# Expert blocks in pairs, register loads by fours, and the planner's charge for a turn set to zero, in a fused cross-attention and mixture-of-experts kernel

## The chip, the cores and the metric

The kernel runs on one core of one Trainium2 chip, in one launch. The metric is device time in microseconds (us). Three runs of the kernel before took 674.27, 676.44 and 676.86 us; the median is 676.44.

## What is computed

2048 tokens of 256 features (fp32) attend to 1601 context rows in 16 heads of 16 features, then go through a mixture of eight experts, two of which serve each token.

```
x = x + xattn(layernorm(x), ctx, ctx, mask)
    q, k, v = query @ Wq.T, key @ Wk.T, value @ Wv.T           # 16 heads, dk = 16
    attn    = softmax(q k^T / 4, masked, causal)
    output  = sigmoid(query @ Wg.T + bg) * (attn @ v) @ Wo.T
x = x + ffn(layernorm(x))
    top 2 of softmax(x @ gate_w) per token give scale[T, 8]
    xs = scale.T[:, :, None] * x                               # (8, T, 256)
    y  = (silu(xs @ w1) * (xs @ w3)) @ w2                      # hidden size 128
    out = y.sum(over experts)
```

## The kernel before, in words

**Attention.** Tokens are worked in four chunks of 512, in the order 1, 2, 3, 0, and each chunk in four groups of four heads; that makes 16 passes n. A pass has three kinds of product on TensorE (PE). *Maximum pieces* (`mx`, L1702, with the causal mask added by small products, L1706) give scores with the queries on the partitions; VectorE (DVE) reduces each to a row maximum (L1392). The maxima of a pass are folded (`mred`, `mT`: POOL, PE, ACT, a small DMA) into an extra row of the queries. *Score products* (`st`, L1735, mask L1740) then give the scores with the keys on the partitions, less the maximum, and ScalarE (ACT) takes their exponential into `probs` (L1267). There are 592. Both kinds run as pairs: two heads in the two halves of PE's rows. *Value products* (`pv`, L1757) take four heads at once, in four strips of 32 columns, and sum over the keys in one bank. A unit is one pass's block of 128 keys; `probs` has room for two units. Of a unit of 512 queries the values are two shares of 256, each of four products.

**Router.** When a chunk's passes are done, `gT`, `wo`, a second layernorm, `xT1` and `logits` (L1585 with `gw_sb`) give the expert scores; DVE ranks them, `cnt` counts rows per expert, `wide` scales each row for its two experts, and POOL scatters the rows into the DRAM table `sent` (`scat`, L1120), sorted by expert. SP writes zero rows behind each expert's last row (`tail`, L986 to L989). Chunks 1, 2, 3 are set 0, chunk 0 is set 1.

**Expert blocks.** 128 rows of one expert are a block: 31 in set 0 and 15 in set 1, 46 in all. Which expert a block belongs to is known only at run time, so SP and PE load it into a register (`value_load`, L1003 and L1824). A block has six steps: `bl`, SP loads the rows (L1004) into one of four places of `row_in`; `bx`, PE transposes them (L1819), ACT copies the high part (L1284), DVE takes the low part (L1548); `bab`, six products with w1 and w3 (L1835 to L1837), ACT takes tanh (L1290), DVE forms the hidden rows (L1554, L1556); `bh`, one transpose (L1843) and again a high and a low part; `by`, three products with w2 (L1849 to L1851), copied out by ACT (L1302); `bst`, SP stores to `fed` (L1010). The steps of four blocks are interleaved by `LAGS`: in round i stand bx(i), bab(i-1), bh(i-2), by(i-3).

**The end.** When all blocks of a set are stored, POOL gathers for each half chunk of 256 tokens the two result rows of every token (`back`, four gathers, L1137) into one of three places `got` in `gate_sb`; DVE adds them to x (`add`, L1569, L1570), and SP stores (`out`, L1015).

**Order.** `make_plan` (L265) walks all steps once with costs in ns, always takes the step that could start first (rounded by TOLERANCE, ties by a deadline in which `PATIENCE` enters), and so writes one list from which each engine takes its own steps in that order. The deciding lines:

```
        if mode != mode_of(e):
            at += SWITCH
...
                key = (max(0, round((at - last) / TOLERANCE)), deadline(name, e, at))
```

The mode is "scores" for `st` and `mx`, "values" for `pv`, "other" for the rest. SP's and POOL's steps are sorted by the times at which the plan has them begin. `needs` lists what each step waits for in the plan.

## Time and profile before

| | |
|---|---|
| median of three runs | 676.44 us |
| profiled execution | 673.26 us, span 671.5 |
| PE busy | 589.1 us, 88% of the span |
| DVE busy | 476.6 us, 71% |
| ACT busy | 382.9 us, 57% |
| POOL busy | 220.0 us, 33% |
| DMA | 51.03 MB, mean 76 GB/s |
| DVE row maxima, L1392 | 323.0 us busy, 640 instructions |
| ACT exponentials, L1267 | 281.7 us busy, 592 instructions |

A busy PE is not PE at its peak: its products overlap, and the end of each is modelled and includes a tail. So distances between the starts of products tell more than their lengths. Idle time of an engine that isn't the bottleneck costs nothing. In the views, PEld is PE's weight load, and a time in brackets is the idle time before an instruction with what released it ("issue": nothing that the profile shows).

### The profile page before, as it was taken

Reading aid. Unit: us, or ns where it says so; the run is one execution under the profiler, and the core shown is the slowest. Engines: PE = TensorE matmul, PEld = TensorE weight load, DVE = VectorE, ACT = ScalarE, POOL = GpSimd, SP = SyncE. Lnnn points to the kernel's source line nnn. Section 1 sums busy time; section 2 is a strip of 40 time slices with the busy share of each in tenths; the row PEclk is TensorE's granted clock in tenths of the full one; section 3 lists DMA queues with packets and bytes.
Section 4 is the critical chain, followed back from the end, with each engine's and each line's share of the span. In section 5 each row is a group of like instructions: output and inputs, shape, how many; then the busy total and the mean of one; then the engine's idle time right before and its main releaser. Section 6 shows DMA issues by size and latency. Waiting matters only on the chain.

```text
span 671.5 us, 14892 instructions
## 1 busy us (share of the span) xinstructions
PE 589.1 (88%) x5272; PEld 353.4 (53%) x5272; DVE 476.6 (71%) x1167; ACT 382.9 (57%) x882; POOL 220.0 (33%) x306
## 2 busy tenths in 40 slices
PE   8896999999999999999999999988898586788750
PEld 3363565555565545554565555533355374777640
DVE  6636779998979999989898896810024678565651
ACT  2221456676656577766756668789977233455430
POOL 6004311432123575030104085477021502100754
PEclk9879799999999999999999899999999799799995
DMA  6985882010170010010087010000000324544873
GB/s 170 231 134 104 142 153 40 2 22 2 65 95 2 2 56 11 1 53 13 3 93 189 3 48 19 4 2 2 1 2 9 134 80 148 177 141 142 223 210 109
DMA packets 43554, 51.03 MB, mean 76 GB/s; under 512 B 8073, under 2 KB 32777, under 8 KB 43482
## 3 DMA queue, kind: packets, MB, share of 16 engines
q1 hardware_dynamic: 37416, 40.50, 26.6%
q0 software_dynamic: 5120, 8.66, 4.5%
q8 instruction: 44, 0.72, 0.5%
q10 hardware_dynamic: 946, 0.92, 0.4%
q14 instruction: 28, 0.23, 0.1%
HBM read 27.41 MB, written 20.58 MB: 71 GB/s over the span
## 4 chain that ended last, share of the span: by engine, by line
PE 27%; DVE 15%; ACT 9%; issue 5%; POOL 3%; DMA 2%; SPq 1%; POOLq 0%; DVEq 0%; ACTq 0%
DVE pmax L1392 9%; ACT probs L1267 7%; PE bank L1757 7%; PE bank L1735 5%; PE bank L1585 3%; PE bank L1702 3%; PE bank L1835 2%; POOL gate_sb L1137 2%; DMA gate_sb<-fed,back_at 1%; PE bank L1837 1%; PE bank L1836 1%; ACT y_sb L1302 1%; POOL sent L1120 1%; DMA fed<-y_sb 1%; PE bank L1706 1%
## 5 line engine op out<-in xcount | busy, mean ns | idle before, releaser
L1267 ACT ACTIVATE probs<-bank 128x512 f32<-128x512 f32 (+4 forms) x592 | 281.7, 560 | 123.9 <-PE bank L1735 77.8
L1392 DVE TENSOR_REDUCE pmax<-bank 128x1 f32<-128x512 f32 (+6 forms) x640 | 323.0, 575 | 29.9 <-PE bank L1706 15.4
L1757 PE MATMUL bank<-probs,vaug 128*32 128x256 f32 (+4 forms) x2048 | 144.5, 394 | 7.9 <-ACT probs L1267 6.3
L1735 PE MATMUL bank<-qaug,kaug 64*128 64x512 f32 (+4 forms) x592 | 146.9, 452 | 2.6 <-DVE pmax L1392 0.9
L1702 PE MATMUL bank<-kaug,qaug 62*128 62x512 f32 (+6 forms) x640 | 137.8, 405 | 10.0 <-ACT rest L1205 4.2
L1735 PEld LDWEIGHTS bank<-qaug,kaug 64*128 64x128 f32 (+1 forms) x592 | 63.8, 183 | 81.1 <-ACT probs L1267 31.6
L1702 PEld LDWEIGHTS bank<-kaug,qaug 62*128 62x128 f32 x640 | 76.9, 190 | 43.2 <-DVE pmax L1392 20.9
L1757 PEld LDWEIGHTS bank<-probs,vaug 128*32 128x32 f32 (+1 forms) x2048 | 52.6, 110 | 60.4 <-ACT probs L1267 26.6
L1137 POOL DMA_INDIRECT gate_sb<-fed,back_at x32 | 31.6, 986 | 59.2 <-DMA fed<-y_sb 46.4
L1835 PE MATMUL bank<-w_hi,row_hi 128*128 x92 | 31.5, 342 | 16.2 <-ACT y_sb L1302 6.5
L1162 POOL DMA_DIRECT2D qaug<-m_row x64 | 34.7, 548 | 31.9 <-ACT m_row L1274 31.9
L1407 DVE TENSOR_SCALAR rsum<-bank 128x16 f32<-128x16 f32 x16 | 2.7, 167 | 53.5 <-PE bank L1767 53.5
L1080 POOL TENSOR_TENSOR rstd<-var_e,minus_half 128x4 f32<-128x4 f32 x8 | 8.3, 1042 | 91.8 <-DVE var_e L1352 91.7
L1706 PE MATMUL bank<-tri_b,eye_b 64*128 64x128 bf16 (+1 forms) x416 | 36.8, 225 | 0.0
L1176 POOL TENSOR_TENSOR att_sb<-att_sb,gate_sb 128x256 f32<-128x256 f32 x16 | 11.7, 731 | 76.2 <-DVE att_sb L1412 75.7
L1290 ACT ACTIVATE t_sb<-bank 128x128 f32<-128x128 f32 x46 | 12.8, 277 | 41.6 <-PE bank L1837 41.6
L1149 POOL TENSOR_SCALAR nmax<-rmax 128x16 f32<-128x16 f32 x16 | 4.4, 277 | 89.9 <-DVE rmax L1400 89.5
L1835 PEld LDWEIGHTS bank<-w_hi,row_hi 128*128 128x128 f32 x92 | 18.3, 199 | 25.8 <-issue 25.7
L1554 DVE SCALAR_TENSOR_TENSOR at_sb<-t_sb,bank 128x128 f32<-128x128 f32 x46 | 13.1, 286 | 24.7 <-ACT t_sb L1290 24.7
L1200 ACT ACTIVATE stage<-bank 128x512 fp32r<-128x512 f32 (+1 forms) x16 | 8.8, 551 | 36.1 <-PE bank L1585 27.9
L1740 PE MATMUL bank<-eye_b,tri_b 64*128 64x64 bf16 (+1 forms) x416 | 27.5, 195 | 0.0
L1284 ACT ACTIVATE row_hi<-bank 128x256 fp32r<-128x256 f32 x46 | 17.4, 380 | 16.8 <-PE bank L1819 16.7
(178 smaller groups left out, 823.2 us busy)
## 6 DMA issues: line engine op xcount, KB each, us to landing
row_in<-sent SPq DMA_DIRECT2D x46, 128.0 KB, 2.1
fed<-y_sb SPq DMA_DIRECT2D x46, 128.0 KB, 2.1
qaug<-q_parts SPq DMA_DIRECT2D x18, 256.0 KB, 8.4
q_parts<-stage SPq DMA_DIRECT2D x7, 512.0 KB, 2.9
sent<-none_sb SPq DMA_DIRECT2D x18, 128.0 KB, 1.8
k_parts<-stage SPq DMA_DIRECT2D x4, 512.0 KB, 5.0
w_sb<-in_w SPq DMA_DIRECT2D x4, 512.0 KB, 10.3
out<-x_sb SPq DMA_DIRECT2D x8, 256.0 KB, 3.2
```

The costliest lines, as they stand in the source:

```text
L1137: pool.indirect_dma_start(got[:, g % GOT, k, t, :], None, rows, bass.IndirectOffsetOnAxis(ap=back_at[:, k, 2 * g + t:2 * g + t + 1], axis= ...
L1162: pool.dma_start(qaug[row:row + 1, p % 2, GP * g:GP * (g + 1), :].bitcast(F32), m_row[at:at + GP, :].bitcast(F32)).then_inc(m_landed[n % 4 ...
L1267: act.activation(probs[0:rows, u % NSLOT, h, off:CH], bank_of(e)[0:rows, off:CH], ACT.Exp, scale=DK ** -0.5).then_inc(act_read, 1)
L1284: act.activation(row_hi[:, i % 2, :], bank_of(e)[:, 0:D], ACT.Copy).then_inc(row_hi_ready, 1)
L1392: dve.tensor_reduce(pmax[:, n % 2, qt, h, slot:slot + 1], bank[:, 0:w], AX_X, ALU.max).then_inc(dve_read, 1)
L1585: last = pe.matmul(dst, lhs(a), rhs(a), start=(a == 0), stop=(a == KD - 1))
L1702: last.append(pe.matmul(pair[side][0][:, 0:w], qaug[b:b + ROW_MAX, p % 2, hp, P * qt:P * (qt + 1)], keys_at(b, ROW_MAX, hp, k0, w), start= ...
L1706: last = [pe.matmul(bank[:, d:w], eye_b[b:b + HALF, a + 1 - side, :], tri_b[b:b + HALF, a + 1 - side, 0:w - d], start=False, stop=(a == 1) ...
L1735: last.append(pe.matmul(pair[side][0][0:r, off:CH], keys_at(b, ROWS, hp, P * j, r), qaug[b:b + ROWS, p % 2, hp, off:CH], start=True, stop= ...
L1740: last = [pe.matmul(bank[0:r, q0:q0 + HALF], tri_b[b:b + HALF, a + 1 - side, 0:r], eye_b[b:b + HALF, a + 1 - side, HALF * a:HALF * (a + 1) ...
L1757: last = pe.matmul(psum[O_BANK][32 * h:32 * h + 32, q0:q1], vaug[0:r, col:col + 32], probs[0:r, u % NSLOT, h, q0:q1], start=(j == 0), stop ...
L1835: pe.matmul(bank[:, 0:D], high, hi, start=(a == 0), stop=False)
```

## The change

- **Blocks in pairs.** Two neighbouring blocks of a set (31 blocks become 15 pairs and a single, 15 become 7 and a single, so 24 steps for 46 blocks) share a bank, a wait and each ACT and DVE instruction. PE's products stay as many. Rings hold two pairs (`RING` = 2), row places `XIN` are two pairs, `YOUT` three pairs. Row places move into `gate_sb`. One store writes both blocks. Row loads stay one per block.
- **Registers by fours.** `named` loads four table entries with one instruction, on SP and on PE, where each block had its own.
- **Gathers.** Four landing places instead of three, in the space of `probs`; the first gather waits for the last value product.
- **Late additions.** `PATIENCE` gets an entry of 30000 for the additions.
- **The planner's costs.** `SWITCH`, the charge for a change of mode, goes from 100 to 0; costs of pairs, of scatters and gathers are new; the weights' split (`ws`) no longer waits in the plan for the last pass's maxima.

```diff
-RELOAD, SWITCH, HOP, LOAD, PIECE = 107, 100, 2500, 9000, 3000
+RELOAD, SWITCH, HOP, LOAD, PIECE = 107, 0, 2500, 9000, 3000
-PATIENCE = {"turn": 1000, "route": 3000, "project": 6000, "weights": 0, "blocks": 4000}
+PATIENCE = {"turn": 1000, "route": 3000, "project": 6000, "weights": 0, "blocks": 4000, "adds": 30000}
-BLOCKS = [(s, b) for s, count in enumerate(COUNT) for b in range(count)]
+PAIRS = [(s, b, min(2, count - b)) for s, count in enumerate(COUNT) for b in range(0, count, 2)]
+NAMED = 4
-XIN, YOUT, GOT = 4, 3, 3
+XIN, YOUT, GOT, RING = 2, 3, 4, 2
-THEN = {"stat": 1050, "mred": 1100, "mT": 2300, "ws": 2700, "gm": 750, "norm": 4900, "scat": 8800, "back": 4400, "wide": 9800}
+THEN = {"stat": 1050, "mred": 1100, "mT": 2300, "ws": 2700, "gm": 750, "norm": 4900, "scat": 10400, "back": 5200, "wide": 9800}
         if kind == "ws":
-            return [("prologue_end",), ("mred", NC * G - 1)] + all_st(freed_by(e[1]))
+            return [("prologue_end",)] + all_st(freed_by(e[1]))
-        got = gate_sb[:, 1:NC, :].rearrange("p g (k t d) -> p g k t d", k=2, t=2)
+        got = words[:, 0:GOT * 4 * D].rearrange("p (g k t d) -> p g k t d", g=GOT, k=2, t=2)
+        row_in = gate_sb[:, ORDER[0], :].rearrange("p (i k d) -> p i k d", i=XIN, k=2)
+        def named(table, s, b, engine, most):
+            count = min(NAMED, COUNT[s] - b)
+            _, values = nc.values_load_multi_w_load_instructions(table[0:1, s, b:b + count], engines=[engine], min_val=0, max_val=most,
+                                                                 skip_runtime_bounds_check_because="the table's values are bounded by its last step")
+            return {(s, b + k): value for k, value in enumerate(values)}
...
+        def landed(i):
+            return row_landed[i % XIN], 16 * sum(PAIRS[o][2] for o in range(i % XIN, i + 1, XIN))
@@ SP, bl @@
                     if i == 0:
-                        sp.wait_ge(*made(last_st[last_unit[G * (NC - 1) - 1]]))
+                        sp.wait_ge(*made(("logits", ORDER[0])))
                     if i >= XIN:
-                        sp.wait_ge(*taken(("bx", i - XIN)))
-                    at = sp.value_load(read_i[0:1, s, b:b + 1], min_val=0, max_val=E * ROOM[s])
-                    sp.dma_start(row_in[:, i % XIN, :], sent[s][bass.ds(at, 1), :, :].rearrange("r p d -> (r p) d")).then_inc(row_landed[i % XIN], 16)
+                        sp.wait_ge(*made(("bx", i - XIN)))
+                    if b % NAMED == 0:
+                        from_row.update(named(read_i, s, b, mybir.EngineType.SP, E * ROOM[s]))
+                    for k in range(n):
+                        sp.dma_start(row_in[:, i % XIN, k, :], sent[s][bass.ds(from_row[s, b + k], 1), :, :].rearrange("r p d -> (r p) d")
+                                     ).then_inc(row_landed[i % XIN], 16)
@@ SP, bst @@
-                    sp.dma_start(fed[s][b, :, :], y_sb[:, i % YOUT, :]).then_inc(y_stored[i % YOUT], 16)
+                    sp.dma_start(fed[s][b:b + n, :, :].rearrange("r p d -> p r d"), y_sb[:, i % YOUT, 0:n, :]).then_inc(y_stored[i % YOUT], 16)
@@ POOL, back @@
                     if g == 0:
-                        for o in ORDER[0:NC - 1]:
-                            pool.wait_ge(*made(("logits", o)))
+                        pool.wait_ge(pv_done, len(units))
@@ ACT, bx; bab, bh and by are changed in the same way @@
-                    act.activation(row_hi[:, i % 2, :], bank_of(e)[:, 0:D], ACT.Copy).then_inc(row_hi_ready, 1)
+                    act.activation(row_hi[:, i % RING, 0:n * D], bank_of(e)[:, 0:n * D], ACT.Copy).then_inc(row_hi_ready, 1)
@@ PE, bab @@
-                    pe.wait_ge(*taken(("bx", i)))
+                    if b % NAMED == 0:
+                        whose.update(named(whose_i, s, b, mybir.EngineType.PE, E - 1))
+                    pe.wait_ge(*taken(("bx", i)))
                     bank = make(e)
-                    for a in range(KD):
+                    for k in range(n):
+                        dst = bank[:, D * k:D * (k + 1)]
+                        for a in range(KD):
...
```

The plan moves the attention's steps against each other. On PE, in the middle of the attention, just ahead of the transposes of the eleventh fold (`nmax_b`), before. Scores and maxima (`kaug` with `qaug`) take two products for a pair, values (`vaug`) four for a share.

```order
L1757 MATMUL bank<-probs,vaug 32x256 x8
L1735 MATMUL bank<-qaug,kaug 128x512 x2
L1702 MATMUL bank<-kaug,qaug 128x364 x4
L1735 MATMUL bank<-qaug,kaug 128x512 x2
L1757 MATMUL bank<-probs,vaug 32x256 x8
L1735 MATMUL bank<-qaug,kaug 128x512 x2
L1702 MATMUL bank<-kaug,qaug 128x512 x4
L1735 MATMUL bank<-qaug,kaug 128x512 x2
L1757 MATMUL bank<-probs,vaug 32x256 x8
L1735 MATMUL bank<-qaug,kaug 128x512 x2
L1702 MATMUL bank<-kaug,qaug 128x364 x4
L1715 MATMUL bank<-eye_b,nmax_b 8x128 x4
```

The same place in the changed kernel (score products are now L1761, maximum pieces L1728 with mask L1732, values L1783):

```order
L1728 MATMUL bank<-kaug,qaug 128x364 x2
L1732 MATMUL bank<-tri_b,eye_b 128x65 x4
L1783 MATMUL bank<-probs,vaug 32x256 x4
L1761 MATMUL bank<-qaug,kaug 128x512 x2
L1728 MATMUL bank<-kaug,qaug 128x512 x2
L1783 MATMUL bank<-probs,vaug 32x256 x4
L1728 MATMUL bank<-kaug,qaug 128x512 x2
L1761 MATMUL bank<-qaug,kaug 128x512 x2
L1728 MATMUL bank<-kaug,qaug 128x364 x2
L1783 MATMUL bank<-probs,vaug 32x256 x4
L1761 MATMUL bank<-qaug,kaug 128x512 x2
L1741 MATMUL bank<-eye_b,nmax_b 8x128 x4
```

The two value shares of a unit are apart now, and maximum pairs stand singly. Over the whole of PE's order the mode changes 557 times where it changed 375 times; 508 of the 592 score products and 896 of the 1024 value products stand ahead of the last maximum piece, where 432 and 748 stood; and behind the logits of chunk 3 stand 12 score products, where 28 stood.

On PE, one round of the expert blocks, before (no row is left out between two register loads):

```order
L1824 TENSOR_LOAD whose_i
L1824 ISA x2
L1835 ISA [waits act_read,dve_read]
L1835 MATMUL bank<-w_hi,row_hi 128x256
L1836 MATMUL bank<-w_hi,row_lo 128x256
L1837 REGISTER_ALU
L1837 MATMUL bank<-w_lo,row_hi 128x256
L1835 ISA
L1835 MATMUL bank<-w_hi,row_hi 128x256
```

and now, where a second pair ends its transposes (the rounds between two such loads have none):

```order
L1847 MATMUL bank<-ident,gate_sb 128x128 [waits dve_read,row_landed1]
L1847 MATMUL bank<-ident,gate_sb 128x128 x3
L861 TENSOR_LOAD whose_i
L1866 ISA [waits act_read,dve_read]
L1866 MATMUL bank<-w_hi,row_hi 128x256
L1867 MATMUL bank<-w_hi,row_lo 128x256
L1868 REGISTER_ALU
L1868 MATMUL bank<-w_lo,row_hi 128x256
L1866 ISA
```

The load of a register (TENSOR_LOAD with two ISA rows) stands once per four blocks, without the two rows behind it.

On SP, in the same stretch, before:

```order
L1003 TENSOR_LOAD read_i [waits dve_read]
L1003 ISA x2
L1004 ISA
L1004 DMA row_in<-sent 128x256
L1010 DMA fed<-y_sb 128x256 [waits act_read]
```

and now, a round with and a round without a register load:

```order
L861 TENSOR_LOAD read_i [waits dve_full]
L1026 ISA
L1026 DMA gate_sb<-sent 128x256
L1026 ISA
L1026 DMA gate_sb<-sent 128x256
L1033 DMA fed<-y_sb 128x2x256 [waits act_read]
L1026 ISA [waits dve_full]
L1026 DMA gate_sb<-sent 128x256
L1026 ISA
L1026 DMA gate_sb<-sent 128x256
L1033 DMA fed<-y_sb 128x2x256 [waits act_read]
```

Two row loads and one store of twice the size stand where two loads and two stores stood, and the loads wait for the transposes (`dve_full`) instead of DVE's copy (`dve_read`).

## Rows read from the trace of the kernel before

**Rows 1.** Windows: length, busy us of each engine, PEclk, DMA share, GB/s.
```profile
300.00:400.00 100.00, 97.32 (x864) 54.22 (x862) 91.38 (x208) 63.12 (x130) 24.84 (x35) 0.98 0.30 58
...
438.00:490.00 52.00, 45.72 (x536) 19.55 (x534) 2.40 (x9) 50.09 (x105) 24.94 (x25) 1.00 0.01 2
...
583.00:617.00 34.00, 29.26 (x215) 25.20 (x214) 21.08 (x72) 19.40 (x72) 0.00 (x0) 1.00 0.46 140
```

**Rows 2.** Page, groups: busy us, mean ns, idle before; the exponentials.
```profile
L1267 ACT ACTIVATE probs<-bank 128x512 f32<-128x512 f32 (+4 forms) x592 | 281.7, 560 | 123.9 <-PE bank L1735 77.8
```

**Rows 3.** Timeline of PE, 243 to 254 us: start, length, instructions.
```profile
244.64 0.49 PE L1735 MATMUL bank<-qaug,kaug 64*128 64x512 f32 x2
245.06 1.07 PE L1757 MATMUL bank<-probs,vaug 128*32 128x256 f32 x16
246.06 0.50 PE L1735 MATMUL bank<-qaug,kaug 64*128 64x512 f32 x2
...
251.41 0.50 PE L1735 MATMUL bank<-qaug,kaug 64*128 64x512 f32 x2
251.75 0.56 PE L1702 MATMUL bank<-kaug,qaug 62*128 62x512 f32 x4
252.18 0.90 PE L1735 MATMUL bank<-qaug,kaug 64*128 64x512 f32 x2
253.08 1.07 PE L1757 MATMUL bank<-probs,vaug 128*32 128x256 f32 x16
```

**Rows 4.** Groups of PE by line, 97 to 438 us.
```profile
L1702 PE MATMUL bank<-kaug,qaug 62*128 62x512 f32 (+6 forms) x560 | 117.3, 396 | 2.4 <-DVE pmax L1392 1.0 <-DVE new_sum L1496 0.4
L1735 PE MATMUL bank<-qaug,kaug 64*128 64x512 f32 (+4 forms) x420 | 113.3, 461 | 2.6 <-DVE pmax L1392 0.9
L1757 PE MATMUL bank<-probs,vaug 128*32 128x256 f32 (+4 forms) x1456 | 101.6, 391 | 0.1
L1706 PE MATMUL bank<-tri_b,eye_b 64*128 64x128 bf16 (+1 forms) x336 | 28.0, 220 | 0.0
```

**Rows 5.** Timelines of DVE at 437 us and of ACT at 525 us.
```profile
437.37 1.29 DVE L1392 TENSOR_REDUCE pmax<-bank 128x1 f32<-128x512 f32 x2 [0.25 <-PE bank L1706]
...
524.73 1.08 ACT L1267 ACTIVATE probs<-bank 128x256 f32<-128x256 f32 x5
```

**Rows 6.** Timelines of PE, POOL and SP, 508 to 536 us.
```profile
508.74 1.95 PE L1585 MATMUL bank<-gw_sb,gate_sb 128*128 128x8 f32 x16
...
522.66 1.16 POOL L1120 DMA_INDIRECT sent<-att_t,slots  x1 [0.26 <-DVE row_sb L859]
...
535.11 11.91 SPq L1004 DMA_DIRECT2D row_in<-sent  x8
```

**Rows 7.** Chain that ended last: start, length, engine.
```profile
584.52 0.38 PE bank L1835
...
607.70 0.37 PE bank L1835
```

**Rows 8.** Timeline of PE and its weight loads, one block.
```profile
590.23 0.38 PE L1835 MATMUL bank<-w_hi,row_hi 128*128 x1 [0.21 <-ACT y_sb L1302]
...
591.49 0.39 PE L1819 MATMUL bank<-ident,row_in 128*128 128x128 f32 x2
...
592.15 0.19 PEld L1835 LDWEIGHTS bank<-w_hi,row_hi 128*128 128x128 f32 x1 [0.52 <-issue]
```

**Rows 9.** Timeline of SP: tail rows written ahead of further loads.
```profile
565.55 8.51 SPq L989 DMA_DIRECT2D sent<-none_sb  x8
```

**Rows 10.** Timelines of POOL (gathers) and SP (last store).
```profile
620.05 0.99 POOL L1137 DMA_INDIRECT gate_sb<-fed,back_at  x1 [45.20 <-DMA fed<-y_sb]
...
655.60 0.94 POOL L1137 DMA_INDIRECT gate_sb<-fed,back_at  x1 [4.84 <-issue]
...
664.64 0.95 POOL L1137 DMA_INDIRECT gate_sb<-fed,back_at  x1 [0.30 <-issue]
...
668.97 0.37 SPq L1015 DMA_DIRECT2D out<-x_sb  x1
```

More of the change, by code:

```diff
@@ L193, in block_steps @@
 def block_steps():
-    steps, count = [], len(BLOCKS)
+    steps, count = [], len(PAIRS)
     for i in range(count + max(LAGS.values())):
@@ L245, in read_time @@
         return per[0] * max_pieces(e[1])[e[2]][3] + per[1]
-    if kind in ("v", "logits", "by"):
+    if kind == "by":
+        return per[0] * PAIRS[e[1]][2] * D + per[1]
+    if kind in ("v", "logits"):
         return per[0] * D + per[1]
@@ L282, in make_plan @@
         "weights": [[("ws", ex)] for ex in range(E)],
-        "loads": [[("bl", i)] for i in range(len(BLOCKS))],
+        "loads": [[("bl", i)] for i in range(len(PAIRS))],
         "blocks": [[e] for e in block_steps()],
-        "stores": [[("bst", i)] for i in range(len(BLOCKS))],
+        "stores": [[("bst", i)] for i in range(len(PAIRS))],
         "backs": [[("back", *o)] for o in halves()],
@@ L462, in alone @@
         if kind in THEN:
[L463 removed]
+            at = on_pool(e, at) + (1.5 * HOP if kind in ("scat", "back") else 60)
         elif kind in ("kload", "qload"):
```

137 lines of the change are left out of this document (77 added, 60 removed).

## The prediction

> **What bounds the kernel now.** I read the windows first, then the timeline of PE, then the chain that ended last. The kernel has two halves. In the attention half (until 526 us) two thirds of the time lie under the row maxima: from 300 to 400 us PE is busy 97.3 of 100 us and DVE 91.4, while ACT, which has all the exponentials, is busy 63.1 [rows 1]. Once the last maximum is taken (DVE, 437 us) ACT alone sets the pace: 50.1 of 52 us busy, DVE 2.4 [rows 1, 5]. So exponentials that could have run under the maxima run behind them, until 526 us [rows 5]. The second half is the expert blocks. From 584.52 to 607.70 twelve blocks pass on the chain, 1.93 us each [rows 7]. PE needs 1.26 us from a block's first product (590.23) to the next transposes (591.49). Of the 0.67 us that remain its weight load stands idle for 0.52, released by nothing but "issue" [rows 8]; I count 0.44 as a gap and 0.23 as the two transposes, so 1.49 of work. The gap lies where PE fetches the block's expert number into a register. From 620 us POOL gathers the results, and the end hangs on its last gather at 664.64 and the last store at 668.97 [rows 10].
>
> **The attention's order.** No instruction of attention is added; the planner's charge for a turn between tilings went from 100 to 0. Counted from the order of instructions, PE has 557 turns where it had 375, and 508 of the 592 score products (148 more of the 1024 value products too) now stand ahead of the last maximum, where 432 stood.
>
> 1. Behind the last maximum ACT has 76 exponentials less, at 0.56 us [rows 2]: -42.5 us.
> 2. Ahead of it PE has 38 score pairs more at 0.34 us (251.41 to 251.75) and 37 groups of four value products at 0.50 (245.06 to 246.06 is two groups) [rows 3]: 12.9 + 18.5 = +31 us.
> 3. A turn: a score pair takes 0.34 us before a maximum and 0.42 before values (244.64 to 245.06) [rows 3], 0.08 more. The turn back is inside the 1.00 us of the values; I take 0.09 for both, 182 x 0.09 = +16 us.
> 4. Two maximum pairs in a row take 0.43 us, 0.215 each, and next to another kind 0.34, the score pair's price [rows 3]; 64 such neighbourhoods are gone: 64 x 0.125 = +8 us.
> 5. Against these 55 us stands the room PE has under the maxima. Between 97 and 438 us, 341 us, stand 182 value groups (eight records each) x 0.50, 210 score pairs x 0.34 and 280 maximum pairs x about 0.27, between 0.215 and 0.34: 238 us [rows 4]. The other groups of that view (the masks on L1706 are the largest) add up to 85 us busy [rows 4], with each one's tail counted; as distances some 60. That leaves about 43 us of waiting; 252.18 to 253.08 shows a piece of it, 0.90 us where 0.42 would do [rows 3]. A new order can use between none and all 43. I take 30, since more alternation gives PE a ready product more often: -30 us.
>
> So the last exponential moves by -42.5 + 55 - 30 = -17.5 us; between the ends of the room from +12.5 to -30.5.
>
> The Trainium skill's page "TensorEngine Tiling (Array Packing)", section Key Properties, says that a change of tiling mode drains TensorE, which speaks against this edit. The page "TensorE: Matmul & The Clock Gate" puts a drain near 175 ns; by it an estimate for item 3 is 32 us in place of 16, and the whole sum would come out 16 us longer.
>
> 6. The way from the router's last big step to the first row load: logits of chunk 3 at 508.74, first scatter 522.66, first row load 535.11 [rows 6]. Before, 28 exponentials stand behind those logits, now 12. The way of 26 us stays as long, and 16 exponentials at about 0.53 us less lie beside it. So row loads come 8 us later after the last exponential: +8 (0 to +9). Queued there are POOL's scatters, SP's tail rows, and all blocks.
>
> Attention together -9.5 us (-30 to +21). The splitting of the expert weights on POOL is moved ahead of several folds; I cost it at nothing, since a fold's maxima lead its scores by 30 or more exponentials, over 15 us. If that cover is gone, PE waits at the first scores of a unit, some 5 us.
>
> **The blocks.** 46 blocks become 24 steps: same products, half of the ACT and DVE instructions, and one register load per four blocks on PE and SP.
>
> 7. A pair costs PE 2 x 1.49 us, and the 0.44 us gap falls on every second pair: 3.18 us where two blocks took 3.86, -0.68. ACT needs at most 2 x 19.4/18 = 2.2 us and DVE 2.3, even unpaired [rows 1]; neither becomes the bound. Set 0 has 15.5 pairs: -10.5 us. Bounds: nothing (the gap only moves), and -13.6 (no gap at all, 15.5 x 0.88).
> 8. SP still puts nine tail writes of set 1, 8.51 us for eight of them [rows 9], ahead of later row loads, and four blocks of row buffers are all the cover as before: 0. The row buffer comes free at its transposes instead of after DVE's copy, and two loads are issued for it instead of one; both beside PE's two steps, so 0, for as long as SP keeps up (a rival below).
> 9. The end. The first gather is at 620.05, the last at 664.64; POOL stands between at 655.60 for the stores of set 1 and for additions [rows 10]. Gathers come every 1.25 us when nothing holds them, 32 of them in all. With four landing places and set 1 ready in time, the last starts at 620.05 + 31 x 1.25 = 658.8: -5.8 us. Set 1 has eight more steps plus a store, about 8 x 3.18 + 3 = 28 us after set 0's last; POOL reaches its gathers 33 us after it. So set 1's blocks hide under the gathers, and so do the late additions; nothing is booked for them. Bounds: 0 and -5.8. What is late next is POOL itself.
>
> Blocks together -16 us (-4 to -19).
>
> **Sum.** -9.5 - 16 = -25.5 us. The profiled execution took 673.26 us with a span of 671.5; the median of the runs shown is 676.44, 3.2 above it. The span should be 646, the profiled time near 648 and the median 651.
>
> **Rivals.**
> *Rows too late.* A pair's loads wait for the transposes two steps back and land some 2 us after issue; if SP, which also stores, comes late, PE waits each step and item 7 is gone: -9.5 - 5.8, 661 us. For it: DMA gaps on PE exist at the blocks' start. Against: two steps of 3.2 us for it, and fewer SP instructions. The same time comes out if the register load simply costs as much on the pairs as before; then the change wouldn't do what it says.
> *No gain in attention.* PE uses only 10 of the 43 us of room: +10.5 - 16, 671 us. For it: PE is busy 97.3 of 100 us already, and the windows can't tell a wait from a product's tail.
> *Turns make PE the bound, slower.* One mechanism: each turn empties the array and nothing overlaps it. Its price at most is the full distance from 0.215 us (a pair in a run) to 0.42: 0.205 a turn, 182 x 0.115 = 21 us more than item 3, and no room used: 12.5 + 21 + 8 - 16 = +25.5, 702 us. At 0.09 a turn it decides only if less than 1 us of room is used (then 681); at 0.205 if less than 22 us is. For it: PE's share. Against: the tight 0.42 in the trace, with the turn in it.
>
> **How the numbers follow.** A measurement of this kernel can tell about 0.5%, 3.4 us, from no change. Forecast 0.58, with its own range of 636 to 664. Late rows 0.12 (661). No gain in attention 0.16 (671, from 666 to 680, so a third of it within 0.5%). Turns 0.12 (680 to 702), nearly all of it slower. Better than forecast (all 43 us of room) 0.02. Faster: 0.58 + 0.12 + 0.08 + 0.02 = 0.80; same 0.08; slower 0.12. The range from 634 to 678 leaves out the turns above 678 and a little below.
>
> **What would show it.** Last maximum near 463 us (later than 437), last exponential near 508, first row load near 526, the chain's blocks 3.2 us a pair with an "issue" gap every second pair, first gather near 600, and 32 gathers without a break longer than 2 us. The forecast is wrong if the last exponential comes later than 520, if the score pair before values takes much over 0.42 us where PE waits for nothing, if a block pair takes over 3.6 us, or if POOL waits on stores of set 1.

## The result, and the profile after

The changed kernel takes 657.06 us (median of 4 runs, 654.97 to 663.90) against 675.36 us before (4 runs, 672.60 to 676.86): ratio 0.9706, interval 0.9647 to 0.9764. It is faster by 18.3 us where 25.4 were forecast. The profiled one of these four runs (663.90 us) was slowed by a lower clock, so the profile read here is that of a second, unaltered run of it (e1 below), with a span of 653.4 us where before had 671.5, and ratios and intervals go by undisturbed runs alone.

The page of it, first parts (columns as for the kernel before):

```profile
span 653.4 us, 14223 instructions
PE 573.5 (88%) x5272; PEld 328.7 (50%) x5272; DVE 473.2 (72%) x1079; ACT 377.8 (58%) x794; POOL 219.6 (34%) x306
PEclk8799999999999799999999889999999869979955
```

PE has the same 5272 products, ACT has 794 instructions. The windows that answer to [rows 1]: a stretch under the maxima, the stretch from the last maximum to the last exponential, and one of steady blocks.

```profile
300.00:400.00 100.00, 95.88 (x862) 48.49 (x858) 84.52 (x187) 67.52 (x131) 38.74 (x45) 0.95 0.32 70
467.60:512.00 44.40, 41.24 (x524) 23.83 (x516) 10.36 (x35) 35.45 (x90) 9.66 (x13) 1.00 0.01 3
583.00:603.00 20.00, 19.82 (x157) 19.21 (x157) 11.48 (x26) 11.65 (x28) 0.00 (x0) 0.94 0.52 164
```

The numbers are those of PE, PEld, DVE, ACT and POOL, then PE's granted clock (PEclk), the DMA share and GB/s. In the second line ACT is busy 35.5 of 44.4 us. Before it had 50.1 of 52: ACT no longer sets the pace alone. In the third, PE is busy 19.8 of 20 us (before 29.3 of 34): PE now bounds the blocks.

The marks of the forecast in the timelines (start, length): DVE's last maximum and ACT's last exponential [rows 5], then logits of chunk 3, first and last of its eight scatters, first row load [rows 6].

```profile
466.66 1.29 DVE L1415 TENSOR_REDUCE pmax<-bank 128x1 f32<-128x512 f32 x2 [0.51 <-PE bank L1732]
...
512.02 0.79 ACT L1289 ACTIVATE probs<-bank 128x128 f32<-128x128 f32 x4 [0.18 <-PE bank L1766]
```
```profile
505.84 1.95 PE L1611 MATMUL bank<-gw_sb,gate_sb 128*128 128x8 f32 x16
...
518.10 1.22 POOL L1143 DMA_INDIRECT sent<-att_t,slots  x1 [1.67 <-DVE row_sb L878]
...
527.23 0.96 POOL L1143 DMA_INDIRECT sent<-row_sb,slots  x1 [0.30 <-issue]
...
530.28 13.63 SPq L1026 DMA_DIRECT2D gate_sb<-sent  x12
```

The last maximum moved from 437.4 to 466.7 us, the last exponential from 525.8 to 512.8, the logits only from 508.7 to 505.8, and the first row load only from 535.1 to 530.3. The 24.4 us between logits and row load (26.4 before) are nearly a fixed way, with hardly anything of the exponentials in it: ACT's one small step there, `r_exp` at 509.82, stands behind four of them that start at 508.32.

Steady blocks, timeline of PE: the first transposes of two steps in a row and the first product of each, then the weight load of a step with a register load in front of it [rows 8]:

```profile
586.30 0.60 PE L1847 MATMUL bank<-ident,gate_sb 128*128 128x128 f32 x4
586.66 0.36 PE L1866 MATMUL bank<-w_hi,row_hi 128*128 x1
...
589.09 0.60 PE L1847 MATMUL bank<-ident,gate_sb 128*128 128x128 f32 x4
589.45 0.36 PE L1866 MATMUL bank<-w_hi,row_hi 128*128 x1
```
```profile
592.21 0.19 PEld L1866 LDWEIGHTS bank<-w_hi,row_hi 128*128 128x128 f32 x1 [0.17 <-issue]
```

A pair takes 2.79 us (586.66 to 589.45) where two blocks took 3.86, and before the weight load 0.17 us is left of the 0.52. But the steps aren't steady all the way. SP's queue between 560 and 600 us, and what PE waits for there (us in total, times, longest), first now, then before:

```profile
568.59 0.41 SPq L1006 DMA_DIRECT2D sent<-none_sb  x1
570.04 8.20 SPq L1009 DMA_DIRECT2D sent<-none_sb  x8
578.91 0.90 SPq L1026 DMA_DIRECT2D gate_sb<-sent  x2
```
```profile
PE bank L1847 <- DMA gate_sb<-sent: 7.4, 2, 7.2
```
```profile
PE bank L1819 <- DMA row_in<-sent: 2.1, 1, 2.1
```

The tail writes of set 1 stand ahead of a row load as in [rows 9]. PE waits 7.2 us for that load, where in the kernel before it waited 2.1. POOL's gathers and the tail of SP's queue [rows 10]:

```profile
606.46 0.99 POOL L1159 DMA_INDIRECT probs<-fed,back_at  x1 [27.45 <-DMA fed<-y_sb]
...
630.51 1.45 POOL L1159 DMA_INDIRECT probs<-fed,back_at  x1 [0.30 <-issue]
...
646.14 0.95 POOL L1159 DMA_INDIRECT probs<-fed,back_at  x1 [0.30 <-issue]
```

They run without the stop of 4.84 us that stood before the 25th. The saving by stretch, from the two traces:

| stretch, us | before | changed | difference |
|---|---|---|---|
| start to first row load | 535.1 | 530.3 | -4.8 |
| first row load to first gather | 84.9 | 76.2 | -8.7 |
| first gather to the end | 51.5 | 46.9 | -4.6 |
| span | 671.5 | 653.4 | -18.1 |

These are single executions. How far a mark moves with nothing changed ahead of it is shown by e5 below: its attention has the order of the kernel before, and its first row load stands at 537.5 us, 2.4 later. So the first line can be told to 2 or 3 us only.

### The profile page after: what moved, and what is told of

It is laid out like the page before. It is cut to its first block, busy times and chain, and to the rows that moved or that the text cites. A ratio compares the mean times of both kernels' runs of the same rounds, so it can differ in the third digit from the quotient of the medians.

```text
span 662.1 us, 14223 instructions
## 1 busy us (share of the span) xinstructions
PE 581.6 (88%) x5272; PEld 332.6 (50%) x5272; DVE 473.3 (71%) x1079; ACT 377.9 (57%) x794; POOL 220.1 (33%) x306
## 4 chain that ended last, share of the span: by engine, by line
PE 65%; DVE 10%; POOL 6%; issue 6%; DMA 4%; ACT 4%; SPq 4%; POOLq 0%; DVEq 0%; ACTq 0%
PE bank L1783 18%; PE bank L1761 13%; PE bank L1728 12%; PE bank L1611 9%; DVE pmax L1415 5%; ACT probs L1289 3%; POOL probs L1159 2%; PE bank L1732 2%; POOL row_sb L1115 1%; PE bank L1866 1%; PE bank L1847 1%; DMA probs<-fed,back_at 1%; PE bank L1868 1%; PE bank L1867 1%; PE bank L1687 1%
## 5 line engine op out<-in xcount | busy, mean ns | idle before, releaser
L1783 PE MATMUL bank<-probs,vaug 128*32 128x256 f32 (+4 forms) x2048 | 161.0, 404 | 3.1 <-ACT probs L1289 1.4
L1761 PE MATMUL bank<-qaug,kaug 64*128 64x512 f32 (+4 forms) x592 | 143.9, 450 | 7.4 <-DVE new_sum L1519 2.7
L1728 PE MATMUL bank<-kaug,qaug 62*128 62x512 f32 (+6 forms) x640 | 140.4, 423 | 3.5 <-DVE stage L889 1.9
L1761 PEld LDWEIGHTS bank<-qaug,kaug 64*128 64x128 f32 (+1 forms) x592 | 64.7, 188 | 77.9 <-DVE pmax L1415 26.1
L1728 PEld LDWEIGHTS bank<-kaug,qaug 62*128 62x128 f32 x640 | 69.9, 190 | 59.4 <-DVE pmax L1415 21.5
L1783 PEld LDWEIGHTS bank<-probs,vaug 128*32 128x32 f32 (+1 forms) x2048 | 46.0, 110 | 54.6 <-issue 26.5
L1159 POOL DMA_INDIRECT probs<-fed,back_at x32 | 31.6, 987 | 36.4 <-DMA fed<-y_sb 27.3
L1732 PE MATMUL bank<-tri_b,eye_b 64*128 64x128 bf16 (+1 forms) x416 | 32.4, 226 | 0.0
L1198 POOL TENSOR_TENSOR att_sb<-att_sb,gate_sb 128x256 f32<-128x256 f32 x16 | 11.8, 737 | 59.4 <-DVE att_sb L1435 57.6
L1306 ACT ACTIVATE row_hi<-bank 128x512 fp32r<-128x512 f32 (+1 forms) x24 | 13.7, 576 | 30.9 <-PE bank L1847 30.8
L1611 PE MATMUL bank<-wo_sb,att_t 128*128 128x256 f32 x64 | 17.2, 418 | 12.7 <-DVE att_t L1404 12.7
L1143 POOL DMA_INDIRECT sent<-att_t,slots x16 | 16.2, 1013 | 31.3 <-DVE row_sb L878 26.8
L1868 PE MATMUL bank<-w_lo,row_hi 128*128 x92 | 26.5, 288 | 0.0
L1867 PE MATMUL bank<-w_hi,row_lo 128*128 x92 | 26.4, 287 | 0.0
L1570 DVE TENSOR_TENSOR row_lo<-bank,row_hi 128x512 fp32r<-128x512 f32 (+1 forms) x24 | 15.9, 665 | 11.5 <-PE bank L1847 6.4
```

Source lines behind the costliest of these rows:

```text
L1159: pool.indirect_dma_start(got[:, g % GOT, k, t, :], None, rows, bass.IndirectOffsetOnAxis(ap=back_at[:, k, 2 * g + t:2 * g + t + 1], axis= ...
L1611: last = pe.matmul(dst, lhs(a), rhs(a), start=(a == 0), stop=(a == KD - 1))
L1728: last.append(pe.matmul(pair[side][0][:, 0:w], qaug[b:b + ROW_MAX, p % 2, hp, P * qt:P * (qt + 1)], keys_at(b, ROW_MAX, hp, k0, w), start= ...
L1732: last = [pe.matmul(bank[:, d:w], eye_b[b:b + HALF, a + 1 - side, :], tri_b[b:b + HALF, a + 1 - side, 0:w - d], start=False, stop=(a == 1) ...
L1761: last.append(pe.matmul(pair[side][0][0:r, off:CH], keys_at(b, ROWS, hp, P * j, r), qaug[b:b + ROWS, p % 2, hp, off:CH], start=True, stop= ...
L1783: last = pe.matmul(psum[O_BANK][32 * h:32 * h + 32, q0:q1], vaug[0:r, col:col + 32], probs[0:r, u % NSLOT, h, q0:q1], start=(j == 0), stop ...
```

## The experiments

Twelve runs were made in three batches, each beside the kernel before (medians 675.32, 675.10 and 675.09 us). The stretches of all of them stand in one table behind the runs; each reading below uses it.

**The changed kernel once more** (e1). No edit.

> The changed kernel unaltered, for a profile whose clock is not disturbed: in the first profile of it PE stood at half clock from 229 to 239 and from 273 to 280 us, in the middle of the attention. Theory (the order of the attention gains a little, the blocks most): 650 to 657 us, last exponential near 513 to 516, first row load near 531 to 533 against 535.1 before, first gather near 607. Rival (the half clock is what the new order brings itself, since PE waits differently): half clock in the attention again, 662 us.

Measured: 657.73 us, ratio 0.9742 (0.9706 to 0.9779). It repeats the result and gives the profile above. The rival's time didn't come, but its half clock did in part: PE's granted clock is at half (1.2 GHz) in this trace too, for 17.1 us between 100 and 467 us (23.9 in the first profile, 3.4 in the kernel before). Windows of 200 to 240 and 350 to 400 us, granted clock in the third number from the end:

```profile
200.00:240.00 40.00, 38.84 (x375) 20.17 (x374) 34.32 (x80) 25.14 (x53) 19.20 (x21) 0.91 0.01 5
350.00:400.00 50.00, 46.24 (x424) 22.40 (x416) 44.96 (x102) 34.38 (x64) 29.05 (x29) 0.90 0.22 65
```

**The order alone, both ways** (e2, e3). The planner's charge for a turn put back in the changed kernel, and taken from the kernel before:

```diff
-RELOAD, SWITCH, HOP, LOAD, PIECE = 107, 0, 2500, 9000, 3000
+RELOAD, SWITCH, HOP, LOAD, PIECE = 107, 100, 2500, 9000, 3000
```

> The changed kernel with the planner's charge for a turn back at 100: PE's order of the attention is again nearly the old one (374 turns, 434 of 592 score products ahead of the last maximum). Theory (items 1 to 6 of the forecast, attention -9.5): 5 to 12 us slower than the changed kernel, 662 to 667, last exponential near 526. Rival 'no gain in attention': within 3 us of the changed kernel. Rival 'turns make PE the bound': faster than the changed kernel.

Measured: 664.12 us, 0.9819 (0.9797 to 0.9841). As the theory said, the order is worth something in the changed kernel: 6.4 us, and the intervals of e1 and e2 don't touch; the first row load is at 537.1 with the old charge and at 530.3 with the new.

> The kernel before with the charge at 0 alone: 552 turns, 516 of 592 score products ahead of the last maximum, blocks single as before. Theory: faster than before by what the order is worth, 5 to 10 us (665 to 670). Rival 'no gain in attention': 673 to 677. Rival 'turns': slower, over 680.

Measured: 680.95 us, 1.0101 (1.0067 to 1.0134). The same number makes the kernel before slower by 5.6 us. That is the time which the rival of the turns gave, but its mechanism isn't what the trace shows. The last exponential does come earlier, 516.8 us instead of 525.8, but the logits of chunk 3 come later, 513.6 instead of 508.7. The chain that ended last says where they were held (start, length, what):

```profile
488.87 1.81 POOL w_lo L1106
490.68 0.77 POOL w_hi L1104
491.61 1.69 issue
493.29 0.73 POOL att_sb L1176
494.07 1.97 PE bank L1775 x8
496.04 3.71 PE bank L1585 x8
```

POOL splits the eight experts' weights (`w_hi`, `w_lo`), and the product that chunk 3's output waits for (`att_sb`, 493.29) stands behind them in its queue. Groups of POOL, 470 to 496 us, of this run:

```profile
L1106 POOL TENSOR_TENSOR w_lo<-w_sb,w_hi 128x768 fp32r<-128x768 f32 x8 | 14.5, 1812 | 0.6
L1104 POOL CAST w_hi<-w_sb 128x768 fp32r<-128x768 f32 x8 | 6.6, 825 | 0.0
```

That is 21 us in one block, 472.0 to 493.3 us, right behind the last maxima. In the kernel before the planner lets no split go ahead of the last pass's maxima; with the old charge these end at 438 us, with the new one at 465. The change drops that rule, and in the changed kernel the splits run at 369.8, 409.5 and 444.5 us, ended by 452.6. DVE had written what that product reads long before:

```profile
476.85 0.42 DVE L1412 TENSOR_TENSOR att_sb<-bank,rinv 128x256 f32<-128x256 f32 x1
```

It waited 16 us behind the splits. In the changed kernel POOL takes the same step at 483.27, 0.1 us after DVE is done with it. The wait also costs clock: the eight products of `wo` behind it take 3.71 us (496.04), and eight of the same kind 1.92 in the changed kernel (488.00). So the forecast's free side edit is, by these traces, what lets the order pay. It is read from the traces; the changed kernel with the old rule wasn't tried, so this is argued and not shown.

**Registers by fours** (e4, e5). Taken from the changed kernel, and given to the kernel before with its single blocks. Core of the first (SP's queue; PE's the same way):

```diff
-                    if b % NAMED == 0:
-                        from_row.update(named(read_i, s, b, mybir.EngineType.SP, E * ROOM[s]))
+                    for k in range(n):
+                        from_row[s, b + k] = sp.value_load(read_i[0:1, s, b + k:b + k + 1], min_val=0, max_val=E * ROOM[s])
```

> The changed kernel with a register load of its own for each block, as before, on SP and PE; pairs stay. Theory (item 7: the gap behind a register load is 0.44 us of every 1.93, and a pair has two of them again): up to 0.88 us per pair and 0.66 more than with one load in four blocks, 15.5 pairs, +5 to +10 us. Rival (the pairs' shared ACT and DVE instructions are what made the step shorter, the register load is hidden): within 2 us of the changed kernel.

Measured: 667.70 us, 0.9874 (0.9845 to 0.9903): 10 us lost, all of it between first row load and first gather (85.7 us against 76.2). Of PE's weight loads after 585 us, this is what one behind the register loads looks like:

```profile
590.11 0.29 PEld L1866 LDWEIGHTS bank<-w_hi,row_hi 128*128 128x128 f32 x1 [1.11 <-issue]
```

Two loads for a pair leave a gap of 1.11 us here (behind a wait, at the lower clock), and between 0 and 1.13 us at the pairs that follow. Core of the second:

```diff
-                    whose[i] = pe.value_load(whose_i[0:1, s, b:b + 1], min_val=0, max_val=E - 1)
+                    if b % 4 == 0:
+                        named_pe.update(named(whose_i, s, b, mybir.EngineType.PE, E - 1))
+                    whose[i] = named_pe[s, b]
```

> The kernel before with its register loads by fours on SP and PE, blocks single, order of the plan as before. Theory (PE's gap behind each register load is what a single block's 1.93 us holds beyond 1.49 of work): blocks of the steady stretch come every 1.5 to 1.6 us, first gather 8 to 12 us earlier, 663 to 668 in all. Rival (the gap is a wait for ACT's or DVE's copies, which only pairs shorten): 1.85 us or more a block, within 2 us of the kernel before.

Measured: 667.85 us, 0.9889 (0.9864 to 0.9914). Every fourth block still has a gap, the three between have none, and blocks come every 1.58 us (19 of them from 581.99 to 612.05) where 1.93 passed before:

```profile
590.14 0.19 PEld L1846 LDWEIGHTS bank<-w_hi,row_hi 128*128 128x128 f32 x1 [0.46 <-issue]
```

Single blocks with loads by fours take 77.8 us from row load to gather, 7.1 less than before; pairs make it 76.2. So of the 8.7 us gained there the loads bring 7.1 and the pairs 1.6. Taken the other way round, pairs without the loads (e4, 85.7) bring nothing over the kernel before (84.9), and the loads then bring 9.5. The gather stretch keeps its stop here (4.29 us ahead of the 25th gather, 51.0 us in all), while e4 has none (48.2 us): it is the pairs that end it, as set 1's blocks then are through at 624 us, before five of the eight additions, and not after 646 (here) or 650 (before).

**The tail writes spread** (e6). In the changed kernel with nothing else altered, SP issues each of the nine tail writes of set 1 behind another load or store:

```diff
             for e in others["sp"]:
+                if e == ("tail", 1):
+                    spread = [("tail_none", 1)] + [("tail_of", 1, ex) for ex in range(E)]
+                    continue
...
+                if spread and e[0] in ("bl", "bst"):
+                    entries.append(spread.pop(0))
```

> The changed kernel with the nine tail writes of set 1 spread over SP's queue, one behind each block entry, instead of standing together for some 10 us ahead of the twelfth pair's row loads. Theory (PE stands 9 us between the ninth and the tenth output copy because SP is behind; the end hangs on POOL's first gather): 5 to 8 us faster than the changed kernel, first gather near 600. Rival (the scatters of set 1 or the half clock hold that stretch): within 2 us.

Measured: 661.25 us, 0.9758 (0.9715 to 0.9801), and the span 653.9 is that of the changed kernel: no gain. SP's queue shows why:

```profile
586.06 1.47 SPq L1020 DMA_DIRECT2D sent<-none_sb  x2
590.46 0.89 SPq L1046 DMA_DIRECT2D gate_sb<-sent  x2
```

The first row load of set 1 (590.46) waits until the last tail write has landed, 2.3 us in SP's waits on `sent<-none_sb`, and by then the writes stand at the pace of the stores between them. The stall moved back by four pairs and fell into pieces: the step there is 5.1 us longer than a pair's 2.8, where the changed kernel has one that is 9.1 longer, and three steps ahead of it are 1.0 to 2.1 us longer.

**The way to the first row load** (e7). One number of the changed kernel: how long the planner may leave the routing work once it is possible.

```diff
-PATIENCE = {"turn": 1000, "route": 3000, "project": 6000, "weights": 0, "blocks": 4000, "adds": 30000}
+PATIENCE = {"turn": 1000, "route": -2000, "project": 6000, "weights": 0, "blocks": 4000, "adds": 30000}
```

> The changed kernel with the plan's patience for the router at -2000 instead of 3000: 36 exponentials stand behind the logits of chunk 3 instead of 12, 554 turns. Theory (item 6: the way from those logits to the first row load, 24.5 us, sets the start of the blocks, so exponentials in front of it are late for nothing): first row load 4 to 10 us earlier than 530.3, total 4 to 8 us faster than the changed kernel. Rival (the logits can't come sooner, PE only waits for them in the queue): within 2 us, or slower.

Measured: 646.89 us, 0.9560 (0.9518 to 0.9602), 10.8 us under the changed kernel, more than the theory gave. Its timelines of PE, ACT and SP:

```profile
492.54 1.95 PE L1611 MATMUL bank<-gw_sb,gate_sb 128*128 128x8 f32 x16
...
513.84 0.79 ACT L1289 ACTIVATE probs<-bank 128x128 f32<-128x128 f32 x4 [0.18 <-PE bank L1766]
...
518.49 11.82 SPq L1026 DMA_DIRECT2D gate_sb<-sent  x10
```

The last exponential is 1.8 us later than in the changed kernel, the logits 13.3 us earlier, and the row load 11.8 us earlier. So it is the logits, and not the last exponential, that the second half starts from. Why the logits come so much earlier is less clear, for the half clock is nearly gone as well (3.4 us between 100 and 467 us, where e1 has 17.1). The two windows of e1, here:

```profile
200.00:240.00 40.00, 39.85 (x400) 21.11 (x399) 36.39 (x82) 27.23 (x57) 23.86 (x29) 1.00 0.09 29
350.00:400.00 50.00, 48.69 (x466) 22.68 (x464) 46.13 (x105) 39.09 (x73) 29.07 (x33) 1.00 0.30 86
```

13.7 us less at half clock are 6.9 us of full-speed work. No run parts this from the patience itself.

**Landing places and late additions** (e8). Three landing places instead of four, and no patience for the additions:

```diff
-XIN, YOUT, GOT, RING = 2, 3, 4, 2
+XIN, YOUT, GOT, RING = 2, 3, 3, 2
```

> The changed kernel with three landing places for gathers and no patience for the additions, as before. Theory (item 9: POOL waits for additions and the blocks' engines wait for gathers; both are worth about 5 us together): gathers with breaks of 2 to 6 us again, 2 to 6 us slower than the changed kernel. Rival (POOL's 1.25 us a gather bounds the end either way): within 2 us.

Measured: 658.21 us, 0.9749 (0.9712 to 0.9786): no difference, as the rival said. First to last gather is 39.8 us in it and 39.7 with four places.

**Does the patience help the kernel before?** (e9, e10). The same number there, alone and with the charge of a turn at 0.

> The kernel before with one number changed: the patience of the routing work in the planner, 3000 to -2000, which brought the changed kernel from 657 to 647 us. Theory 1 (in both kernels the end hangs on the logits of chunk 3 by a fixed chain of about 25 us to the first row load, and the patience only sets how early those logits come): the logits come at about 497 instead of 508.7, the first row load at about 523 instead of 535.1, and the time is 664 to 667 us. Theory 2 (only an order that takes the exponentials early has the room for it; here the last exponential at 525.8 still holds the first row load): the logits come early, the row load stays near 533, and the time is 672 to 676 us.

Measured: 674.51 us, 0.9984 (0.9958 to 1.0010). The second theory fits the time: nothing is gained. But its reason doesn't: logits come at 507.1, only 1.6 us earlier. The chain that ended last shows what holds them in this order:

```profile
479.42 1.92 ACT probs L1267 x4
481.38 1.92 ACT probs L1267 x4
483.35 1.98 ACT probs L1267 x4
485.86 1.30 ACT probs L1267 x3
487.30 0.64 ACT o_sb L1255
```

The exponentials themselves, one behind the other. The theory's half about early logits was wrong: they can't come early, since the output of chunk 3 needs exponentials that the old order has piled up behind the last maximum.

> The kernel before with both numbers of the planner changed: patience of the routing work -2000 and price of a turn 0. Alone, the price of 0 cost this kernel 5.6 us (680.95), its last exponential came 9 us earlier (516.8) and its logits of chunk 3 came 5 us later (513.6). Theory 1 (what the order gives was locked behind late logits): with the logits early the order pays, and this is 5 to 7 us below the run with the patience alone, 658 to 662 us. Theory 2 (the turns themselves cost what the order gives): it is 3 to 6 us above that run, 668 to 675 us.

Measured: 677.29 us, 1.0020 (0.9991 to 1.0050). The first theory is refuted. The 2.8 us above e9 don't show the second, since the two intervals overlap. In this order too the turns aren't what the logits wait for: the chain goes through POOL, where the splits end only at 495.2:

```profile
492.57 0.78 POOL w_hi L1104
493.42 1.51 POOL w_lo L1106
495.17 2.12 POOL qaug L1162 x4
497.31 0.75 POOL att_sb L1176
```

**Both numbers in the changed kernel** (e11). Patience -2000, charge 100.

> The changed kernel with patience -2000 for the routing work and the old price of a turn, 100. The price alone cost it 6 us (664.1), the patience alone gave 11 us (646.9). Theory 1 (the two are separate terms): 664.1 - 10.8 = 653 us, row load 6 us later than the 518.5 of the run with the patience alone. Theory 2 (both act on the same chain, and the early logits give all of it): 647 to 649 us, the order is worth nothing more.

Measured: 661.60 us, 0.9789 (0.9750 to 0.9828). Neither theory: 8.6 us above the first, some 13 above the second. With the old charge the patience is worth 2.5 us by the medians, which isn't clear of noise (the interval of e2 is 0.9797 to 0.9841); with the new one it is worth 10.8. The four runs on either kernel, medians in us and ratios to the kernel before:

| | charge 100 | charge 0 |
|---|---|---|
| before, patience 3000 | 675.1 (1) | 681.0 (1.0101) |
| before, patience -2000 | 674.5 (0.9984) | 677.3 (1.0020) |
| changed, patience 3000 | 664.1 (0.9819) | 657.7 (0.9742) |
| changed, patience -2000 | 661.6 (0.9789) | 646.9 (0.9560) |

By the chains read above, three things lie one behind the other ahead of chunk 3's logits: exponentials left over, weights' splits on POOL, and the planner's leave to wait. Taking one away shows the next; only where all three are gone does the row load move by 17 us.

**Tail writes from POOL** (e12). The e7 kernel, with the tail writes of set 1 issued by POOL behind its scatters of chunk 0:

```diff
+                    if c == SETS[1][-1]:
+                        pool.wait_ge(tail_ready, 2)
+                        pool.dma_start(sent[1][E * ROOM[1], :, :], none_sb[:, :]).then_inc(tail_out[1], 16)
+                        for ex in range(E):
+                            at = pool.value_load(tail_at[0:1, 1, ex:ex + 1], min_val=0, max_val=P * E * ROOM[1] - P)
...
```

> The changed kernel with patience -2000, and the nine tail writes of set 1 issued by POOL's queue behind its scatters of chunk 0, no longer by SP's. Theory 1 (SP's queue holds the row loads of the pairs for the 9 us that the nine issues take, and PE idles): the 9 us between by(8) and by(9) go, first gather at about 588 instead of 596.4, time 637 to 640 us. Theory 2 (as when the same writes were spread over SP's queue, which gave nothing: the stall only moves to the first row load of set 1, which waits for the last tail write to land): by(9) comes early, a stall of 6 to 9 us stands ahead of the pairs of set 1, the time is 645 to 648 us.

Measured: 643.70 us, 0.9505 (0.9454 to 0.9556). The interval overlaps that of e7 (0.9518 to 0.9602), so the times alone don't settle 3 us; the traces do agree on it (first gather 592.4 against 596.4, span 639.7 against 643.5). POOL's writes, SP's loads around set 1's first, and PE's waits for rows from 560 to 600 us:

```profile
567.54 4.32 POOL L1150 DMA_DIRECT2D sent<-none_sb  x8
```
```profile
570.54 0.38 SPq L1033 DMA_DIRECT2D fed<-y_sb  x1
576.52 0.85 SPq L1026 DMA_DIRECT2D gate_sb<-sent  x2
```
```profile
PE bank L1853 <- DMA gate_sb<-sent: 3.4, 2, 2.5
```

The longest wait for rows, 7.6 us in e7 (7.2 in e1), is down to 2.5, and a new gap stands in front of set 1's first load. About half of the first theory's gain came (the first gather 4.0 us earlier of 8.4). It is the fastest kernel run here, 31 us under the one before.

Stretches of all runs, us of one profiled execution each:

| run | last maximum | last exponential ends | logits of chunk 3 | first row load | load to first gather | gather to end | span |
|---|---|---|---|---|---|---|---|
| before | 438.0 | 525.8 | 508.7 | 535.1 | 84.9 | 51.5 | 671.5 |
| e1 changed | 467.3 | 512.8 | 505.8 | 530.3 | 76.2 | 46.9 | 653.4 |
| e2 | 444.0 | 527.4 | 511.4 | 537.1 | 78.4 | 47.8 | 663.3 |
| e3 | 465.2 | 516.8 | 513.6 | 538.0 | 85.3 | 51.9 | 675.2 |
| e4 | 467.8 | 513.3 | 506.3 | 531.6 | 85.7 | 48.2 | 665.5 |
| e5 | 441.0 | 527.8 | 511.8 | 537.5 | 77.8 | 51.0 | 666.3 |
| e6 | 466.9 | 512.4 | 505.5 | 529.9 | 77.2 | 46.8 | 653.9 |
| e7 | 469.7 | 514.6 | 492.5 | 518.5 | 77.9 | 47.1 | 643.5 |
| e8 | 467.4 | 513.0 | 506.0 | 530.4 | 75.8 | 47.0 | 653.2 |
| e9 | 440.5 | 523.0 | 507.1 | 533.0 | 86.7 | 51.3 | 671.0 |
| e10 | 472.0 | 530.0 | 515.9 | 541.2 | 86.9 | 51.1 | 679.2 |
| e11 | 441.1 | 525.5 | 508.2 | 535.2 | 77.0 | 47.2 | 659.4 |
| e12 | 469.1 | 513.9 | 493.3 | 517.3 | 75.1 | 47.3 | 639.7 |

From logits to row load it is 24.0 to 27.0 us in all thirteen, while from the end of the last exponential to the row load it is between 3.4 and 21.2.

The time at half clock between 100 and 467 us goes partly with the order. With charge 0 and patience 3000 it is 17.1 us in e1, e4, e6 and e8, 23.9 in the first profile and 13.7 in e3. With charge 100 it is 3.4 (before), 6.8 (e2) and 13.7 (e5), so it also differs between runs of one order. With patience -2000 it is 0 to 6.8 us in all four (e7 and e9 to e11) and 3.4 in e12.

## Why the prediction was right, and where its steps missed

The sign and the range were right, and each half lies in its own range: -9.5 and -16 us forecast, -4.8 and -13.3 measured. (The range of the blocks, -4 to -19, doesn't follow from its items, whose bounds add up to 0 and -19.4.) None of its signs of being wrong came: the last exponential ends at 512.8 and not after 520, a pair takes 2.79 us and not over 3.6, and a score pair before values takes no more than 0.43 us where PE goes from one to the other without a wait. By its steps:

- **Items 1 to 4** (exponentials, moved products, turns, broken runs). From the last maximum to the end of the last exponential it is 87.8 us before and 45.5 now: -42.3 for the forecast's -42.5. The last maximum moved by 29.3 us for 55 less the room used. So if the 55 us are right, 25.7 us of room were used and not 30 (item 5), and the last exponential moved by 13.0 us, not by 17.5. Where those 4.3 us went may be in two windows of the changed kernel: from 200 to 240 us PE's granted clock was 0.91, from 350 to 400 us 0.90, where the kernel before has 1.00 and 0.97. That is 40 x 0.09 + 50 x 0.10 = 8.6 us of full-speed work lost against 50 x 0.03 = 1.5. For it speaks e5, with the old order and 10.3 us more at half clock than the kernel before: its last maximum is 3.0 us later. Against it speaks e7, whose clock is full in both windows and whose last maximum is at 469.7, though in a third order. That this is the cause is argued, not shown. Items 2 to 4 weren't measured apart. In item 5 the other groups add up to 94 us busy and not to 85; by the same share that leaves some 36 us of room and not 43, of which 25.7 were used.
- **The drain of a turn.** The estimate by the Trainium skill's page "TensorE: Matmul & The Clock Gate", section "Single matmul latency", would have put 16 us more on the sum. With it the last maximum would stand near 479 us, and it stands at 467. The trace speaks against that price for a turn, unless 42 of the 43 us of room were used (and there were some 36, as said above).
- **Item 6** (the way to the row load, +8). The row load stands 17.5 us behind the last exponential, where it stood 9.3: +8.2. The size was right in part by luck: the logits stand 7.0 us before the end of the last exponential where they stood 17.1, which is 10.1 us of delay, and the way behind them got 2.0 us shorter instead of staying as long. The picture fell short too. The item took the time of the logits from the last exponential; e7 and the table show that the two move apart (e3: exponential 9.0 us earlier, logits 4.9 later). The last exponential came 13.0 us earlier, the logits 2.9, and it is these that the second half got.
- **The splitting of the weights "at nothing".** This step of the forecast failed. It asked only whether the splits delay PE's scores, and not what their old place would do in the new order. The new charge with the old rule is e3, slower by 5.6 us: its logits come at 513.6, those of the changed kernel at 505.8. If nothing else of the change moves them, the dropped rule is worth those 8 us, more than the 6.4 that the order brought. With the charge at 100 it shows no such worth: logits at 507.1 with the old rule (e9) and at 508.2 with the new (e11). No run has the rule alone.
- **Item 7** (a pair at 3.18 us). It takes 2.79. The gap of the register load goes nearly whole (0 to 0.27 us left), and the two steps in one take less than 2 x 1.49. The sum of -10.5 stands beside -10.8 for first transposes to set 0's last result (77.4 us before, 66.6 now), but this agreement is luck: the steady steps gained more than forecast, while the start lost 4.9 us (first result 11.7 us behind the first transposes, 6.8 before, since it stands behind eight row loads instead of four), which the forecast hadn't. The cause was right: the item got its -0.68 us from register loads saved, and by e4 and e5 it is the loads by fours that bring 7 to 10 us there, the pairs between -0.8 and 1.6.
- **Item 8** (tail writes, 0). The stall is there in both, but not equally long: PE's wait for rows is 7.2 us where it was 2.1 (3.3 us of waiting for DVE stood just ahead of it there), and the longest step takes 9.1 us more than a pair, where two steps took 4.1 and 3.0 more than a block. So some 2 us of cost were put at nothing. The 7.2 us are the largest single wait left in the blocks.
- **Item 9** (gathers, -5.8). -4.9 from first to last gather (44.6 to 39.7); one gather took 1.45 us instead of 0.95 (630.51), another (615.28) is 0.2 us longer, and the rest is rounding of the intervals. That POOL is the bound of the end is shown by its gathers, one every 1.25 us without a break, and by e8: places and late additions change nothing. The gain comes from set 1's blocks being through early.
- **The rivals.** Rows too late is refuted in the steady stretch, where PE is busy 19.8 of 20 us; it holds only at the tail writes, as before. No gain in attention was to use 10 us of room and bring +10.5; 25.7 were used if the 55 us are right, and the row load came 4.8 us earlier, so it is refuted, though half of the forecast gain stayed out. Turns as the bound are refuted by e2 against e1; e3, which has their time, has another cause.

## What to carry to other kernels

An order's worth can't be read from the engine that it relieves: follow the chain from the point where the next stage starts, here the logits, backwards, and ask of each queue on it what stands ahead there. Two edits of which each loses or brings nothing alone (680.95 and 674.5 us against 675.1) can bring the most beside others, so a planner's costs are to be tried in combination, with the marks of the trace beside the time. A register load in every step on PE cost each step about half a microsecond here: try loading several with one instruction before merging the steps themselves. And compare the granted clock of the same stretches before crediting an order with what two traces differ by.

## What the runs showed of the hardware

- **Register loads on PE.** One per block leaves its weight load idle for 0.43 to 0.69 us in the steady blocks before (0.52 in [rows 8]), two in a row for up to 1.13 us (e4). One instruction for four registers leaves 0.26 to 0.70 us on every fourth single block and nothing on the others (e5), and 0 to 0.27 us where pairs stand beside it. So a load of four costs about as much as a load of one. Why it leaves less beside pairs isn't shown.
- **The granted clock after a wait.** Windows of PE alone behind the 7.2 us wait that ended at 581.78 us (length, busy, clock, DMA share, GB/s):

```profile
582.50:585.30 2.80, 2.80 (x15) 0.50 0.55 168
585.50:589.30 3.80, 3.80 (x34) 1.00 0.39 125
```

  The products come 0.21 us apart in the first (1.2 GHz) and 0.12 apart in the second (2.4 GHz). So this wait also slowed what followed it. The same holds for the 16 products of L1611 at 530.87 us: behind a wait of 13.1 us they took 5.40 us, and 16 of the same shape in e9 (L1585, 493.96), where PE had been busy, 3.67. They stand ahead of the first transposes of the blocks (536.10), so this slowness lies on the way to the blocks. The Trainium skill's page "TensorE: Matmul & The Clock Gate", section "HAM oscillation — how this bites in real kernels", describes how a wait for a transfer leaves the next products at the lower clock, and the trace agrees. Not every fall follows a wait, though: in e1 the clock is at half from 213.4 to 220.2 us, and in the 10.4 us before PE was busy 10.2.
- **The same writes from another queue.** Eight writes of 128 KB with a register load each took SP 8.20 us to issue (570.04; 8.51 in [rows 9]) and POOL 4.32 us (567.54, e12), one execution each.
